# Last conditioning set in seven block products, a wait for each token operand, and fewer operands made

## The reference

```
hidden = relu(x @ wi.T + 2 * lora_common + 2 * lora_expert[id])      # 256 -> 1024
y      = hidden @ wo.T + 2 * lora_common + 2 * lora_expert[id]       # 1024 -> 256
```

```
probs = softmax(mean_over_tokens(y) @ gate_w);  top_w, top_i = top_k(probs, 2);  top_w /= sum(top_w)
out   = x + sum over the 2 picks of top_w * (gelu(y @ w1[e] + b1[e]) @ w2[e] + b2[e])
```

## Time and profile before

| what | value |
|---|---|
| median of 3 runs | 265.77 us |
| the runs | 265.80, 265.77, 264.86 us |
| span of the profiled execution | 263.6 us |
| PE busy | 259.6 us, 98% |
| DVE, ACT, POOL busy | 172.6, 174.8, 165.2 us |
| matmuls | 1158 |

### The profile page before, as it was taken

How to read it: one execution, slowest core, us unless ns; L and a number is a source line. 1 busy time by engine, 2 the same in 40 slices (tenths; PEclk the granted TensorE clock), 3 DMA queues, 4 the chain that set the end, 5 groups by cost and what they waited for, 6 DMA issues and landing times.

```text
span 263.6 us, 3639 instructions
## 1 busy us (share of the span) xinstructions
PE 259.6 (98%) x1158; PEld 211.6 (80%) x1158; DVE 172.6 (65%) x287; ACT 174.8 (66%) x281; POOL 165.2 (63%) x198
## 2 busy tenths in 40 slices
PE   8999999999999999999999999999999999999995
PEld 3788888888888788888888888888888888888884
DVE  0772867385997845757594866658856567665665
ACT  2757365468634299878977887676777677775650
POOL 2267997966677977897549999456366366331100
PEclk9999999999999999999999999999999999999999
DMA  6995120201033202211203112202202205000004
GB/s 199 365 357 185 42 80 0 85 1 40 2 120 81 63 16 83 80 39 42 83 0 75 50 37 80 81 0 82 79 3 80 79 3 200 0 0 2 0 1 159
DMA packets 11235, 19.60 MB, mean 74 GB/s; under 512 B 2000, under 2 KB 2640, under 8 KB 11088
## 3 DMA queue, kind: packets, MB, share of 16 engines
q1 hardware_dynamic: 10640, 18.45, 21.5%
q10 hardware_dynamic: 576, 0.92, 1.1%
HBM read 17.26 MB, written 2.10 MB: 73 GB/s over the span
## 4 chain that ended last, share of the span: by engine, by line
PE 97%; DMA 1%; SPq 1%; DVE 0%; issue 0%
PE hid_ps L780 14%; PE hid_ps L781 14%; PE hid_ps L784 14%; PE out_ps L780 12%; PE out_ps L781 12%; PE out_ps L784 12%; PE out_ps L789 4%; PE out_ps L790 4%; PE out_ps L793 4%; PE hid_ps L826 2%; DMA first_rows<-in_early 1%; PE hid_ps L793 1%; PE hid_ps L790 1%; PE hid_ps L789 1%; SPq L338 1%; PE hid_ps L977 1%
## 5 line engine op out<-in xcount | busy, mean ns | idle before, releaser
L424 POOL TENSOR_TENSOR up_lo<-up_raw,up_hi 128x512 fp32r<-128x512 f32 x42 | 54.2, 1312 | 30.0 <-ACT up_hi L594 27.3
L626 ACT ACTIVATE hid_ps<-hid_ps,bias_sb 128x512 f32<-128x512 f32 x64 | 42.2, 659 | 29.2 <-DVE hid_ps L1155 18.0
L780 PE MATMUL hid_ps<-act_hi,up_hi 128*128 128x512 f32 x157 | 61.4, 391 | 0.0
L781 PE MATMUL hid_ps<-act_lo,up_hi 128*128 128x512 f32 x157 | 61.2, 390 | 0.0
L784 PE MATMUL hid_ps<-act_hi,up_lo 128*128 128x512 f32 x157 | 61.1, 389 | 0.0
L1129 DVE SCALAR_TENSOR_TENSOR hid_lo<-hid_ps,mix,hid_hi 128x512 fp32r<-128x512 f32 x64 | 47.9, 748 | 20.2 <-ACT hid_hi L640 19.7
L780 PE MATMUL out_ps<-hid_hi,down_hi 128*128 128x512 f32 x144 | 56.2, 390 | 0.0
L781 PE MATMUL out_ps<-hid_lo,down_hi 128*128 128x512 f32 x144 | 56.1, 389 | 0.0
L784 PE MATMUL out_ps<-hid_hi,down_lo 128*128 128x512 f32 x144 | 56.0, 389 | 0.0
L430 POOL TENSOR_TENSOR down_lo<-down_raw,down_hi 128x512 fp32r<-128x512 f32 x24 | 32.0, 1332 | 33.3 <-ACT down_hi L604 33.2
L640 ACT ACTIVATE hid_hi<-hid_ps,mix 128x512 fp32r<-128x512 f32 x64 | 44.1, 689 | 4.7
(11 more groups left out here) (110 smaller groups left out, 330.8 us busy)
## 6 DMA issues: line engine op xcount, KB each, us to landing
up_raw<-in_w SPq DMA_DIRECT2D x16, 256.0 KB, 2.8
down_raw<-in_w SPq DMA_DIRECT2D x16, 256.0 KB, 2.6
lora_raw<-in_lora SPq DMA_DIRECT2D x8, 256.0 KB, 4.9
down_raw<-in_woT SPq DMA_DIRECT2D x8, 256.0 KB, 3.6
up_raw<-in_wiT SPq DMA_DIRECT2D x7, 256.0 KB, 4.8
outT<-x_sb SPq DMA_DIRECT2D x6, 256.0 KB, 3.5
x_sb<-in_x1T SPq DMA_DIRECT2D x1, 1024.0 KB, 7.9
x_sb<-in_x0bT SPq DMA_DIRECT2D x1, 512.0 KB, 5.8
```

Of the source, the lines that this page charges most:

```text
L424: ins = eng.tensor_tensor(up_lo[:, n, cols], up_raw[:, n, cols], f32(up_hi[:, n, cols]), ALU.subtract)
L626: eng.activation(hid_ps[:, j, :], hid_ps[:, j, :], ACT.Gelu, bias=bias_sb[:, b, k, f:f + 1])\
L780: eng.matmul(out, w_h, a_h, start=start, stop=False, skip_group_check=onto)
L781: eng.matmul(out, w_h, a_l, start=False, stop=False, skip_group_check=onto)
```

## The change

The diff, with all its parts that alter work, order or waits; what is left out are declarations of semaphores and blank lines.

```
-    PLAIN = [n for n in range(N_COND) if n not in (SETS, SETS + 1, SETS + 2)]
+    PLAIN = list(range(SETS))
+    RAW_OPERANDS = (0, 2, 3)
-    RAW_LO_AT = {2: [(0, 0), (0, 1), (0, 2), (0, 3)], 7: [(1, 0), (1, 1)],
-                 11: [(2, 0), (2, 1)], 12: [(2, 2), (2, 3)]}
+    RAW_LO_AT = {2: [(0, 0), (0, 2), (0, 3)], 7: [(1, 0)], 11: [(2, 0)], 12: [(2, 2), (2, 3)]}
-    SUM_LO_AT = {..., 7: [(1, 0), (1, 1), (1, 2), (1, 3)], 13: ..., 14: ...}
+    SUM_LO_AT = {..., 7: [(1, 2), (1, 1), (1, 0)], 8: [(1, 3)], 13: ..., 14: ...}
         # raw_low and sum_low: then_inc on a semaphore for each operand m;
         # sum_low waits for its own s_sum_hi[m // 2]
         # token_sum, for every m and not only the first of a stage:
+                if p:
+                    eng.wait_ge(s_sum_lo[m], p)
 # POOL
                 elif q == 5:
                     ...
                     up_low(6)
-                    token_sum(1, 1)
+                    weight_sums(7)
                     down_low(5)
                 elif q == 6:
                     eng.wait_ge(s_pick, TOP_K)
+                    up_low(7)
+                    token_sum(1, 1)
                     token_sum(1, 2)
+                    down_low(6)
                     token_sum(1, 3)
-                    up_low(7)
-                    raw_low(eng, 1, 2)
-                    raw_low(eng, 1, 3)
-                    down_low(6)
                 elif q == N_COND - 1:
                     weight_sums(q + 1)
+                    raw_low(eng, 1, 2)
                     up_low(q + 1)
+                    weight_sums(q + 2)
                     down_low(q)
-                    weight_sums(q + 2)
+                    raw_low(eng, 1, 3)
                     up_low(q + 2)
 # ACT: raw_high rounds only the blocks in RAW_OPERANDS (block 1 no longer)
                     if seven(q):
+                        if q == 6:
+                            up_high(7)
+                        elif q == 7:
+                            sum_high(1, 1)
+                            up_high(8)
                         hid_high(q, 1)
-                        if q == 5:
-                            up_high(7)
-                        elif q == 6:
-                            sum_high(1, 1)
+                        if q == 7:
+                            sum_high(1, 0)
                         hid_high(q, 2)
                         down_high(q)
-                        if q == 5:
-                            sum_high(1, 0)
 ...
                     gelu(q, 0)
                     hid_high(q, 0)
-                    if q - 1 in GROUP_LAST[0:NB]:
-                        cond_out(GROUP_LAST.index(q - 1), 0)
                     if q + 2 < NSET and q not in EXP_AT:
                         up_high(q + 2)
                     gelu(q, 1)
                     hid_high(q, 1)
+                    if q - 1 in GROUP_LAST[0:NB]:
+                        cond_out(GROUP_LAST.index(q - 1), 0)
 # PE: operands(q) keeps only its wait for up_hi; ahead of each block product
+            def token_side(q, a):
+                if q in GROUP_FIRST[1:]:
+                    eng.wait_ge(s_raw_lo[a] if a < 4 else s_sum_lo[a - 4], GROUP_FIRST.index(q))
 # DVE, sets of seven among the conditioning sets
+                    one_low(RAW_LO_AT, q, 0, raw_low)      # ahead of third_sum
                     third_sum(q)
                     hid_low(q, 0)
+                    one_low(SUM_LO_AT, q, 0, sum_low)
                     ...
                     hid_low(q, 2)
+                    one_low(SUM_LO_AT, q, 1, sum_low)
+                    one_low(SUM_LO_AT, q, 2, sum_low)
 # DVE, from set 8 on
                 hid_low(q - 1, 3)
+                if q == N_COND:
+                    one_low(SUM_LO_AT, q, 0, sum_low)
                 third_sum(q)
```

More of the change, by code:

```diff
@@ L193, in build @@
         s_prod0 = sem("s_prod0")
-        s_r1, s_gelu, s_hid_hi, s_up_hi, s_down_hi, s_y, s_raw_hi, s_sum_hi, s_lhi, s_exp = (
-            sem(n) for n in ("s_r1", "s_gelu", "s_hid_hi", "s_up_hi", "s_down_hi", "s_y", "s_raw_hi", "s_sum_hi",
+        s_r1, s_gelu, s_hid_hi, s_up_hi, s_down_hi, s_y, s_raw_hi, s_lhi, s_exp = (
+            sem(n) for n in ("s_r1", "s_gelu", "s_hid_hi", "s_up_hi", "s_down_hi", "s_y", "s_raw_hi",
                              "s_lhi", "s_exp"))
+        s_sum_hi = [sem(f"s_sum_hi{n}") for n in range(2)]
         s_x0hi, s_up0hi = sem("s_x0hi"), sem("s_up0hi")
-        s_r2, s_r3, s_add, s_hid_lo, s_merge, s_raw_lo, s_sum_lo, s_fin, s_final, s_last = (
-            sem(n) for n in ("s_r2", "s_r3", "s_add", "s_hid_lo", "s_merge", "s_raw_lo", "s_sum_lo", "s_fin", "s_final",
-                             "s_last"))
+        s_r2, s_r3, s_add, s_hid_lo, s_merge, s_fin, s_final, s_last = (
+            sem(n) for n in ("s_r2", "s_r3", "s_add", "s_hid_lo", "s_merge", "s_fin", "s_final", "s_last"))
+        s_raw_lo = {m: sem(f"s_raw_lo{m}") for m in RAW_OPERANDS}
+        s_sum_lo = [sem(f"s_sum_lo{m}") for m in range(4)]
         s_up0lo, s_merge0, s_tok = sem("s_up0lo"), sem("s_merge0"), sem("s_tok")
@@ L287, in raw_low @@
             eng.tensor_tensor(act_lo[:, b, m, :], raw_tile(p, m // NT, m % NT), f32(act_hi[:, b, m, :]),
[L288 removed]
+                              ALU.subtract).then_inc(s_raw_lo[m], 1)
         def sum_low(eng, p, m):
             b = READY_SEQ[p]
[L292 removed]
+            eng.wait_ge(s_sum_hi[m // 2], p + 1)
             eng.tensor_tensor(act_lo[:, b, 4 + m, :], t_sum[:, m, :], f32(act_hi[:, b, 4 + m, :]),
[L294 removed]
+                              ALU.subtract).then_inc(s_sum_lo[m], 1)
         def raw_tile(p, kd, t):
@@ L556, in _ @@
                         raw_low(eng, p, m)
-                    for p, m in SUM_LO_AT.get(q, ()):
-                        sum_low(eng, p, m)
+                    if q > N_COND:
+                        for p, m in SUM_LO_AT.get(q, ()):
+                            sum_low(eng, p, m)
                     if q + 2 < NSET and q not in EXP_AT:
@@ L648, in cond_out @@
                     eng.wait_ge(s_t, 8)
-                    eng.wait_ge(s_raw_lo, 8)
+                    for m in RAW_OPERANDS:
+                        eng.wait_ge(s_raw_lo[m], 2)
                 for kd in range(KD):
@@ L655, in raw_high @@
                 b = READY_SEQ[p]
+                halves = sum(m // NT == kd for m in RAW_OPERANDS)
                 if p == 0:
                     eng.wait_ge(s_x1, 16)
-                    src = x_sb[:, 1, :, kd, :]
+                    src = x_sb[:, 1, 0:halves, kd, :]
                 else:
@@ L661, in raw_high @@
                     eng.wait_ge(s_up, ups_before(SETS * p))
-                    src = y_sb[:, kd, :].rearrange("p (t c) -> p t c", c=TOK)
-                eng.activation(act_hi[:, b, kd * NT:(kd + 1) * NT, :], src, ACT.Copy).then_inc(s_raw_hi, 1)
+                    src = y_sb[:, kd, 0:halves * TOK].rearrange("p (t c) -> p t c", c=TOK)
+                eng.activation(act_hi[:, b, kd * NT:kd * NT + halves, :], src, ACT.Copy).then_inc(s_raw_hi, 1)
             def sum_high(p, n):
@@ L881, in one_of_seven @@
                     bank_free(q, bank)
+                token_side(q, OPERANDS[what][1])
                 up_product(q, *OPERANDS[what], bank, start, True, first_low(q) if what == "m1" else None,
@@ L1134, in second_sum @@
                 n = sevens_before(q)
-                if n and (cond(q) or q in COPY_AHEAD):
+                if n and (q <= N_COND or q in COPY_AHEAD):
                     eng.wait_ge(s_add, 3 * n)
```

7 lines of the change are left out of this document (2 added, 5 removed).

## The result

| | before | changed |
|---|---|---|
| median, 6 runs each | 265.12 us | 267.37 us |
| lowest to highest | 264.86 to 265.80 | 267.17 to 267.70 |
| span of the profiled execution | 263.6 us | 265.4 us |
| in it, from the first router logit to the second | 54.65 us | 56.66 us |
| in it, from the second router logit to the end | 144.56 us | 144.56 us |

The change makes the kernel 0.7% slower. The whole loss lies between the two router logits of sets 5 and 10; behind the second one the two executions take the same time to 0.01 us. (A stretch is read from the first matmul behind one logit to the first behind the other.) The page of the changed kernel gives PE three matmuls less and a chain that no longer runs in PE alone; the first line is busy time by engine, the second the chain that ended last.

A forecast was written before the change was run, and what follows sets the result against it. PE was taken to bound the kernel, busy for 259.6 of 263.6 us. Terms -0.68 - 0.20 + 0.44 + 1.1 + 1.4 = +2.06 us on 265.77 gave 267.8 us, 0.8% slower, range 264.8 to 268.7 us.

The forecast's parts named there:

- The hand-over: Price assumed throughout for passing a result from another engine to PE, read at set 8's start: 0.29 us.
- (a): Set 7 on PE: 21 up matmuls instead of 24, a gain of 0.68 us.
- (b): Start of set 8 on PE: it starts on token block 0 alone, so the wait goes, gaining 0.20 us.
- (c): One raw block less on ACT, DVE and POOL, off the path: gain 0, bounds 0 and 0.1.
- Stall 1: Set 6: router shares caught by POOL's `up_low(7)` delay the first tile sum and PE's m3, 0.44 us.
- Stall 2: Set 8: PE waits for `down_low(7)` from POOL, delayed by collisions with DVE's low parts, 1.1 us.
- Stall 3: Sets 8 and 9: late `weight_sums(10)` hold ACT's `up_high(10)`, so PE waits for set 9's first copy, 1.4 us.
- the spare 0.24: Set 9: margin between ACT's first copy and PE's m2 in the kernel before, 0.24 us.
- (1): Sets 6 to 8: POOL 1.6 us faster than counted, only the gains left, 264.9 us; chance 0.20.
- (2): Only ACT's copy for set 9 is late, POOL about 0.6 ahead of the count, 266.0 us; chance 0.24.
- (3): Start of set 8: the last operand wasn't what held it, 0.2 less gain; chance inside the other cases.
- (4): DVE and POOL collisions cost the whole instruction, 1.2 us more in sets 8 and 9, 269.0 us; chance 0.06.

The follow-up runs named there:

- the kernel with `up_high(8)` first: The two moves plus `up_high(8)` ahead of `sum_high(1, 1)` on ACT and `sum_low(1, 2)` behind the second tile sum on DVE: 264.61 us, ratio 0.9964.
- the last experiment: Kernel before, set 7 plain, with each product waiting for its own token operand and `weight_sums(9)` ahead of `down_low(7)` on POOL: 265.39 us, ratio 0.9989.
- the two moves: Changed kernel with the router's shares at the end of set 6 and `weight_sums(10)` directly behind `down_low(7)`: 265.43 us, ratio 0.9992.
- the tighter fit: The three moves plus `raw_low(1, 2)` on DVE, `up_high(8)` ahead of `sum_high(1, 1)`, `sum_low(1, 2)` behind the second tile sum: 265.87 us, ratio 1.0019.
- the three moves: Changed kernel with the router's shares at the end of set 6, `weight_sums(10)` behind `down_low(7)`, and `sum_low(1, 0)` in set 8: 265.49 us, ratio 0.9999.
- one collision less: Changed kernel with only `sum_low(1, 0)` moved from the end of set 7 into set 8: 267.54 us, ratio 1.0071.

## Why the prediction was right

**The sum.** Forecast +2.06 us; the waits and gains in the trace give +2.02, the ratio +1.8 (1.5 to 2.2). The two medians of six lie 2.25 us apart, more than the ratio gives, but the kernel before had medians of 265.52 to 265.61 in the three later rounds, so its 265.12 is low by almost half a microsecond. The time forecast, 267.8, is 0.4 over the median, and the mis-sized term is the 2.2 us that I put between span and time: I took the median of three runs less the span of one. Every run on record has its time 1.7 to 1.9 us above its own span (267.17 against 265.4), and 263.6 + 2.06 + 1.8 is 267.5.

**The hand-over.** The 0.29 us that I used throughout is too long. After each of the four waits PE's first matmul starts 0.05 to 0.06 us behind the end of what it waited for (78.14 to 78.19, 94.04 to 94.10, 103.44 to 103.50, 106.21 to 106.26); with the late second start that makes 0.17. In the kernel before, PE's queue still passed another wait, at 91.38, and began to load weights at 91.46, between the end of the low part at 91.20 and the start at 91.49, so that distance isn't the price of one wait.

**The gains.** (a) Three matmuls less: shown, 1155 against 1158, and set 7 lasts 90.85 - 80.38 = 10.47 us, 46 slots of 0.2275. (b) 0.20: right in the changed kernel, for a reason I had not given. The next thing due, the first copy of set 8, stands behind the same weight sums as before; it stayed hidden only because PE waited for `down_low(7)` in between. (The copy ends at 93.94, and without the wait PE would want it near 93.6.) Once POOL is early enough it needs no such cover: in the kernel with `up_high(8)` first, which has no wait on `down_low(7)`, the sums end at 91.28 and the copy at 92.86, and m2 of set 8 isn't late. For a plain set 7 the last experiment shows the same, with the sums ahead of `down_low(7)`. (c) 0 for the operands left out: shown from the second router logit on, where the two kernels are equal.

**Stall 1**, 0.44 forecast, 0.35 measured; the hand-over, 0.29 against 0.17, accounts for it (0.32 with 0.17). The chain is the one described: the first tiny instruction (L1192, now L1205) caught for 1.18 us, both shares caught, the tile sum at 77.45 where 77.61 was forecast.

**Stall 2**, 1.1 forecast, 1.10 measured, by the mechanism forecast: POOL without pause, four collisions of 0.41 to 0.45 ahead of the end of `down_low(7)`, at 94.04 where I had 94.2. The agreement to the hundredth is luck: the hand-over was 0.12 too long, and PE wanted the operand 0.3 us earlier than I had (93.12 against 93.4), of which only 0.19 is the earlier start of this execution. The loss of stall 1 is part of it: with the shares moved it falls to 0.63.

**Stall 3**, 1.4 forecast, 1.45 measured. The cause is right: sums at 100.23 (100.3 forecast), ACT idle 1.90 us (1.7). In the size two errors of 0.2 us meet: ACT was that much later, and the spare 0.24, counted with a hand-over of 0.29, was 0.47 with 0.06. The place is half right. I let PE meet only the first copy; half of it is taken earlier, at m6 of set 9, by the low part of set 8's second tile, which hangs on the same late ACT. The same omission made me misjudge the kernel with `cond_out` back.

**The rivals.** (1) and (2) needed POOL 1.6 and 0.6 us earlier; it was 0.1 to 0.2 earlier, no more than this execution's earlier start. (3) fell: m1 was freed. (4), the whole instruction as POOL's loss, asked for 0.68 a collision; the five measured in the changed kernel are 0.41 to 0.51. That is also where the Trainium skill (SBUF — State Buffer, "Who interferes with whom") and the trace part: its rule that two SBUF inputs on DVE and a reading GpSimd instruction exclude each other, and one input doesn't, holds for the low parts, the two caught shares and the reciprocal here, and for DVE's sums with one operand in PSUM (0.68 to 0.70 throughout); that the loser is fully blocked while the other has the pair, for its whole instruction, would be more than POOL lost.

**What stays open.** The kernel with `up_high(8)` first is in one comparison only. That its gain over the two moves comes of where the low parts fall, and would change with another alignment, is read from one profiled execution, which shows only 0.43 us of the 0.7 that the ratios give. The same holds for the tighter fit, slower than the three moves by its ratio and level with them in the trace.

## What to carry to other kernels

Where one engine is full, a change that saves it 0.7 us is worth only what the hand-written order of the others lets through: write out the queue of the engine that gets the new work, over the sets behind it too, with each wait for another engine's result in it, before believing that the work is hidden. An instruction on another engine's critical queue may be cover for a wait (taking it away won nothing) and a collision avoided in one place is paid in the next unless the instruction moves to where there is slack. And the same change, with four reorderings (the shares, the weight sums, `up_high(8)`, one low part), is 0.4% faster than the kernel before by its ratio (0.2 to 0.5) and 0.65 us shorter between the logits: the edit was sound, its place in the queues was not.

## What the runs showed of the hardware

- DVE and POOL meet not only at semaphores: they alternate. A DVE instruction with two SBUF operands waits for the POOL instruction in progress and then goes ahead of the next one in POOL's queue; POOL loses 0.41 to 0.51 us for a DVE instruction of 0.68 (the five of the changed kernel). Two such in a row on DVE against POOL instructions of 1.25 us take 2.52 to 3.11 us (three moves, tighter fit, one collision less) instead of 1.28, and against 128x128 ones 1.55 to 1.57.
- Size doesn't protect: a 128x1 sum and a 128x1 product of two tensors, 0.15 and 0.16 us alone, took 0.85 and 1.02. A reciprocal between them, with one input, took its 0.16.
- A wait on PE costs more than its length: the first matmul starts 0.05 to 0.06 us behind the end of what it waited for, and the start behind it is 0.10 to 0.12 late again (the four waits of the changed kernel).
